# Attention of a two-layer kernel: an order written by hand gives way to a list scheduler, units of 512 queries and heads that share a bank

## The reference, cut to what matters

```python
q = _apply_rotary(q, cos, sin)
k = _apply_rotary(k, cos, sin)
attn = jnp.einsum('bhqd,bhkd->bhqk', q, k) * scale
allowed = (j <= i) & (i - j < WINDOW)
attn = jnp.where(allowed, attn, -jnp.inf)
attn = jax.nn.softmax(attn, axis=-1)
out = jnp.einsum('bhqk,bhkd->bhqd', attn, v)
```

## Time and profile before

| | |
|---|---|
| median of 3 runs | 2544.14 us (2537.84 to 2553.32) |
| the profiled execution | 2542.74 us, span 2541.0 us |
| TensorE busy | 1949.2 us, 77% of the span |
| VectorE, ScalarE, GpSimd busy | 1188.7, 837.3, 476.4 us |
| mean granted TensorE clock | 0.888 |
| the five attention stages | 1366.15 us, 54% of the span |

### The profile page before, as it was taken

The page is one execution under the profiler, slowest core; times in us unless marked ns, Lnnn a source line. Parts: engine busy times, 40 slices in busy tenths (PEclk is TensorE's granted clock), DMA queues, the critical chain, the costliest instruction groups (busy, mean ns, idle before and its releaser), DMA issues. The chain is left out here.

```text
span 2541.0 us, 32056 instructions
## 1 busy us (share of the span) xinstructions
PE 1949.2 (77%) x11444; PEld 1189.2 (47%) x11444; DVE 1188.7 (47%) x2913; ACT 837.3 (33%) x1671; POOL 476.4 (19%) x543
## 2 busy tenths in 40 slices
PE   5777688877667888767769797686797299999991
PEld 3455333345453333445433344564334266666660
DVE  4447666444656764436667543476774100000114
ACT  1332155533221645332126453221365122222212
POOL 4120211010202011103110110211100423333321
PEclk9889799988787999878889998797999599999995
DMA  6400330341003304410023123102210423333315
GB/s 162 52 2 1 66 43 10 51 51 34 2 2 65 51 1 52 51 35 1 26 41 51 25 34 46 34 0 46 30 27 1 145 63 70 70 69 67 69 19 145
DMA packets 91693, 115.01 MB, mean 45 GB/s; under 512 B 19616, under 2 KB 64864, under 8 KB 91376
## 3 DMA queue, kind: packets, MB, share of 16 engines
q1 hardware_dynamic: 76688, 96.07, 19.7%
q0 software_dynamic: 14848, 16.85, 4.0%
HBM read 40.72 MB, written 21.38 MB: 24 GB/s over the span
## 5 line engine op out<-in xcount | busy, mean ns | idle before, releaser
L419 ACT ACTIVATE b_probs<-b_psum 128x512 f32<-128x512 f32 (+3 forms) x768 | 348.7, 494 | 244.4 <-PE b_psum L363 237.9
L509 DVE TENSOR_REDUCE b_mneg<-b_psum 128x1 f32<-128x384 f32 (+3 forms) x512 | 240.7, 486 | 139.9 <-PE b_psum L341 135.4
L341 PE MATMUL b_psum<-b_qk 96*128 96x512 bf16 (+3 forms) x768 | 253.2, 350 | 40.1 <-DVE b_v L470 21.6
L538 POOL TENSOR_TENSOR b_rot<-b_product 128x128 f32<-128x128 f32 x256 | 111.3, 461 | 860.0 <-DVE b_product L464 860.0
L363 PE MATMUL b_psum<-b_qk 99*128 99x512 bf16 (+3 forms) x768 | 238.7, 332 | 10.4 <-DVE b_v L470 6.5
L504 DVE TENSOR_REDUCE b_mneg<-b_psum 128x2 f32<-128x384 f32 (+1 forms) x256 | 138.0, 541 | 228.6 <-PE b_psum L334 223.2
L391 PE MATMUL b_psum<-b_probs,b_v 128*32 128x192 f32 (+5 forms) x2688 | 235.5, 427 | 0.3
L1203 PE MATMUL b_psum<-b_w,b_hid 128*128 128x256 f32 x1024 | 222.4, 379 | 0.8 <-ACT b_hid L1227 0.8
L1248 DVE TENSOR_TENSOR b_ye<-b_psum,b_b2b 128x512 f32<-128x512 f32 x32 | 22.1, 692 | 428.9 <-PE b_psum L1203 390.5
L1194 PE MATMUL b_psum<-b_xgt,b_w 128*128 128x512 f32 x512 | 221.6, 593 | 0.0
L306 PE MATMUL b_psum<-b_wqkv,b_xt 128*128 128x384 f32 x512 | 204.9, 529 | 5.6 <-PEq L850 4.7
(11 more groups left out here) (201 smaller groups left out, 2939.8 us busy)
## 6 DMA issues: line engine op xcount, KB each, us to landing
b_qk<-b_split SPq DMA_DIRECT2D x324, 128.0 KB, 6.5
b_w<-in_W SPq DMA_DIRECT2D x16, 1024.0 KB, 7.0
b_qk<-b_split SPq DMA_DIRECT2D x120, 64.0 KB, 2.6
b_src<-in_x SPq DMA_DIRECT2D x4, 1024.0 KB, 5.5
normed<-b_probs SPq DMA_DIRECT2D x4, 1024.0 KB, 4.7
before_last_norm<-b_x SPq DMA_DIRECT2D x4, 1024.0 KB, 7.1
b_rows<-before_last_norm SPq DMA_DIRECT2D x8, 512.0 KB, 7.2
out<-b_rows SPq DMA_DIRECT2D x8, 512.0 KB, 3.0
```

The lines of the kernel that those rows point to most:

```text
L341: ins = pe.matmul(r[:, 0:e - a], q[0:KS, h, P * t:P * t + P], q[0:KS, HG + h, a:e], start=not last, stop=True, skip_group_check=True)
L419: act.activation(u.probs[t % 2][:, heads[0], a:e], u.psum[:, plan.bank[x], 0:e - a], ACT.Exp, scale=SCALE).then_inc(s.exp_done, 1)
L509: ins = dve.tensor_reduce(out, u.psum[:, plan.bank[x], 0:e - a], AX.X, ALU.max, negate=True)
L538: ins = pool.tensor_tensor(out[:, :, :, HALF * y:HALF * y + HALF], straight[:, :, :, HALF * y:HALF * y + HALF], crossed[:, :, :, HALF * (1 ...
```

## The change

A class `Plan` takes the place of `Script`. Its `describe` lists every step with its engine, a cost in us and the steps it waits for. `arrange` then plays these costs forward in time when the kernel is built: whenever an engine is free, it takes, among the kinds of step whose next one is ready, that with the longest chain of costs behind it. Each engine gets its own order (`plan.program`), and a step gets the bank that is free first, out of five (0, 1, 2, 3, 7). The costs are constants in the text, a DMA lands 3.0 us after its issue, and a wait across engines is 0.12 us.

Further: maxima, rows, exponentials, values and collect go by units of 512 queries (g, h) instead of a whole group; pieces of 128 columns hold four heads and pieces of 256 columns two, so that a causal group has 38 pieces for max and 38 for exp; a windowed group gets 9 cells and 18 pieces for exp instead of 8 and 16. The turned values share bank 6, two tiles at a time, where they had two banks and four tiles. The maxima of a unit go by one DMA from 12 rows. v has room for six groups, `mrow` and `mparts` are double; some small buffers of `route` now lie in `u.qk[1]`.

```diff
+    BANKS = (0, 1, 2, 3, 7)
+    TAKEN_BY = {"proj": "rotate", "fetch": "refill", "max": "reduce", "rows": "lines", "exp": "power", "out": "divide",
+              "back": "keep"}
+    LANDING = 3.0
...
+    def query_cells(self, g, h):
+
+        w = self.windowed[g]
+        return [(t, max(P * t, BANK * h), min(BANK * (h + 1), P * t + WQ if w else T))
+                for t in range(NT) if max(P * t, BANK * h) < min(BANK * (h + 1), P * t + WQ if w else T)]
+    def pieces(self, g, a, e):
+
+        n = 2 if self.windowed[g] else 4 if e - a <= P else 2 if e - a <= 2 * P else 1
+        return [(tuple(range(k, k + n)), a, e) for k in range(0, HG, n)]
...
+                add(("proj", j, t), "PE", 0.66, name("refill", 1, NC - 1) if j >= NG // 2 else None,
+                    name("load", 2 * j - 1, 1, 5, None) if t == 0 else None)
+                add(("rotate", j, t), "DVE", 0.98, ("proj", j, t), name("add", *divmod(n - 2, NT)) if n >= 2 else None,
+                    name("values", 2 * j - 5, 1, NT - 1) if j >= 3 else None)
+                add(("add", j, t), "POOL", 0.88, ("rotate", j, t), name("turn", *divmod(n - 2, NT)) if n >= 2 else None)
+                add(("turn", j, t), "PE", 0.25, ("add", j, t), name("rest", *divmod(n // 2 - 1, 4)) if t % 2 == 0 and n else None)
...
+        def load(g, y=None):
+            last = ("power",) + self.last_piece(g - 3, 1) if g >= 3 else None
+            q = 3 if y is None else 2 * y + 1
+            for part, kind in enumerate(("high", "mid", "low")):
+                for a in range(2):
+                    for slot in SLOTS_OF[a][part]:
+                        add(("load", g, a, slot, y), "SP", 0.46 if y is not None else 0.64, (kind, g // 2, q), last)
...
+                        add(("max", g, t, x), "PE", 0.03 + n * (w + (w if windowed[g] else P if mask else 0)) * 0.00042, y, z)
+                        add(("reduce", g, t, x), "DVE", 0.16 + n * w * 0.00103, ("max", g, t, x),
+                            name("parts", g - 1, h))
+            add(("parts", g, h), "DVE", 1.1, name("reduce", g, 4 * h + 3, self.pieces(g, *self.key_spans(g, 4 * h + 3)[-1])[-1]),
+                name("rows", *before(mine, 2)) if before(mine, 2) else None)
+            add(("rows", g, h), "PE", 0.25, ("parts", g, h))
+            add(("lines", g, h), "ACT", 0.6, ("rows", g, h), name("spread", *before(mine, 2)) if before(mine, 2) else None)
+            add(("spread", g, h), "SP", 0.5, ("lines", g, h))
...
+                    add(("exp", g, h, t, x), "PE", 0.03 + n * (w + (w if windowed[g] else P if mask else 0)) * 0.00042,
+                        ("spread", g, h))
+                    add(("power", g, h, t, x), "ACT", 0.18 + n * w * 0.00085, ("exp", g, h, t, x),
+                        name("values", *self.cells[i - 4]) if i >= 4 else None)
+                add(("values", g, h, t), "PE", 0.1 + (e - a) * 0.0017, ("power", g, h, t, x), name("collect", g - 1, h))
+            add(("collect", g, h), "ACT", 0.62, ("values", g, h, cells[-1][0]), name("out", g - 1, h))
+            add(("out", g, h), "PE", 0.45, ("collect", g, h))
+            add(("divide", g, h), "DVE", 0.75, ("out", g, h))
...
+            urgent[x] = st.cost + max([urgent[y] for y in followers[x]], default=0)
...
+        while left:
+            soonest, moved = None, False
+            for engine, lists in queues.items():
+                at = free_at.get(engine, 0.0)
+                best = None
+                for (q,) in lists:
+                    if not q:
+                        continue
+                    x = q[-1]
+                    if any(y not in done for y in steps[x].after):
+                        continue
+                    ready = max([done[y] + (0.0 if steps[y].engine == engine else self.LANDING if steps[y].engine == "SP"
+                                            else 0.12) for y in steps[x].after], default=0.0)
+                    if x[0] in self.TAKEN_BY:
+                        b = min(bank_free, key=lambda k: bank_free[k])
+                        ready = max(ready, bank_free[b])
+                    start = max(at, ready)
+                    if start > now:
+                        soonest = start if soonest is None else min(soonest, start)
+                    elif best is None or urgent[x] > urgent[best[0]]:
+                        best = (x, q)
+                if best is not None:
+                    x, q = best
+                    q.pop()
+                    left -= 1
+                    moved = True
+                    end = now + steps[x].cost
+                    free_at[engine] = done[x] = end
+                    self.program[engine].append(x)
+                    if x[0] in self.TAKEN_BY:
+                        b = min(bank_free, key=lambda k: bank_free[k])
+                        self.bank[x], self.after[x] = b, used.get(b)
+                        used[b] = x
+                        bank_free[b] = float("inf")
+                    if x in issue_of:
+                        bank_free[self.bank[issue_of[x]]] = end + 0.12
...
+    def in_bank(x, heads, w):
+
+        n = len(heads)
+        return u.psum[:, plan.bank[x], :].rearrange("p (h w) -> p h w", h=n)[:, :, 0:w]
...
-                    for j in range(3):
-                        sp.dma_start(u.qk[g % 3][KS + j:KS + j + 1, 0:HG, :].rearrange("o h (t q) -> o (h t) q", q=P),
-                                     u.mrow[32 * j:32 * j + 32, :]).then_inc(s.m_rows, 16)
+                    sp.dma_start(u.qk[g % 3][KS:KS + 3, 0:HG, BANK * h:BANK * h + BANK], u.mrow[n % 2][0:3 * HG, :]
+                                 ).then_inc(rows_sent[n % 2], 16)
...
+                    elif last:
+                        pe.matmul(out[:, :, P * t - a:P * t - a + P], u.id16[:, :],
+                                  u.causal_q[:, :].unsqueeze(1).broadcast_to([P, len(heads), P]), start=True, stop=True,
+                                  skip_group_check=True)
+                    for i, h in enumerate(heads):
+                        ins = pe.matmul(out[:, i, :], q[0:KS, h, P * t:P * t + P], q[0:KS, HG + h, a:e],
+                                        start=not last, stop=True, skip_group_check=True)
...
-    sbuf(nc, ctx, u, "v", [P, NG, NT, HG * (HD + 1) + 15])
+    sbuf(nc, ctx, u, "v", [P, 6, NT, HG * (HD + 1) + 15])
```

More of the change, by code:

```diff
@@ L232, in wait_bank @@
         y = self.after[x]
         if y is not None:
-            eng.wait_ge({"max": s.max_read, "exp": s.exp_done, "out": s.out_read, "proj": s.pj_read,
-                         "rows": s.rows_read, "fetch": s.fetched, "back": s.back_read}[y[0]], self.order[y] + 1)
+            pe.wait_ge({"proj": s.pj_read, "fetch": s.fetched, "max": s.max_read, "rows": s.rows_read, "exp": s.exp_done,
+                        "out": s.out_read, "back": s.back_read}[y[0]], self.order[y] + 1)
+SLOTS_OF = (((0, 1, 2), (3, 4), (5,)), ((0, 3, 5), (1, 4), (2,)))
@@ new lines, in rows_bank, with split_of, turned_bank, probs_of @@
+    def rows_bank(x):
+        return u.psum[:, plan.bank[x], :].bitcast(BF16)[0:3 * HG, 0:BANK]
+    def split_of(q, part):
+        return u.split[:, :, part, 2 * P * q:2 * P * q + 2 * P]
+    def turned_bank():
+        return u.psum[:, 6, :].rearrange("p (a x) -> p a x", a=2)
+    def probs_of(cell):
+        i = plan.cells.index(cell) % 4
+        return u.probs[i // 2][:, :, BANK * (i % 2):BANK * (i % 2) + BANK]
+    def unit_number(g, h):
+        return 2 * g + h
+    def load_done(eng, g, y=None):
+        if g:
+            eng.wait_ge(loaded[g], 16 * 2 * SLOTS)
+        else:
+            for n in range(2) if y is None else (y,):
+                eng.wait_ge(loaded[groups + n], 16 * 2 * SLOTS)
@@ L293, in _ @@
+            for n in range(2):
+                sp.wait_ge(rows_sent[n], 16 * groups)
             sp.wait_ge(later, 16 * len(LATER_WEIGHTS))
@@ L401, in _ @@
                     ins.then_inc(s.out_ready, 1)
+                elif kind == "back":
+                    y = x[2]
+                    pe.wait_ge(s.out_read, order[("divide", g + 1, y)] + 1)
+                    for t in range(4):
+                        ins = pe.transpose(u.psum[:, plan.bank[x], P * t:P * t + P], o_of(g)[:, 4 * y + t, 0:P], u.id32[:, :])
+                    ins.then_inc(s.back_ready, 1)
         @block.scalar
         def _(act):
-            for x in plan.steps:
+            for x in plan.program["ACT"]:
```

603 lines of the change are left out of this document (294 added, 309 removed).

## The result

The changed kernel takes **2340.8 us**, the median of 3 runs (2339.49 to 2347.63), where the kernel before took 2544.14. The ratio is 0.9205, with a 95% interval of 0.9152 to 0.9257: 203 us less, 8%. The profiled execution has a span of 2337.7 us (2541.0 before), a mean granted TensorE clock of 0.898 (0.888) and TensorE busy for 1912.0 us (1949.2).

What follows compares the result with a forecast made beforehand. Nothing was saturated: a joint stage needs about 224 us of TensorE and 117 are waiting. Savings of 134 us in three joint stages, 11 in the last and 19 in the first sum to 164, giving 2380, range 2265 to 2500.

Steps and rivals of the forecast that it cites:

- The head, 52: Start of a joint stage: first maxima at 22 us, first exponential at 52 us, 5 earlier than before.
- Group 0, to 99: First causal group of a joint stage: 37.7 us of work plus gaps of 0.25 a pair, 47 us.
- Group 1, 36 us, to 135: Second causal group of a joint stage: 29.2 us of work plus 38 gaps of 0.17 us, 36 us.
- Group 2, 53 us, to 188: Joint-stage group with fetch and pair 2: 43.1 plus 9.5 us, 53, where it was 65.4 with a stall of 8.33.
- The rest, 110: Joint stage after group 2: 130.9 us falls to 110, losing the 11.92 stall and about 9 through moved projections.
- Stages: Attention stage lengths: joint 298 us against 342.8 in the mean, last 193 (11 less), first 115 (19 less).
- causal groups over 45 us: Sign of being wrong: causal groups in the changed profile still taking over 45 us each.
- Outside the stages: Sign of being wrong: stages between the attention stages changing length at all.
- my lower rival, in which the gaps close further: Attention stages: five banks and planned order leave no gap, 2207 us, or about 2290 with half the gaps; chance 0.15.
- Pieces that share a bank: Causal groups: 38 pairs of max and exp pieces in place of 48, 1.7 us a group at 0.17 a pair.
- The rival of shrunken gain: Attention stages: wrong planner prices leave gaps and half the load stalls, 72 us gained, 2470 us; chance 0.17.
- The slower rival: Rows on SyncE stand behind late loads, 2656 us if all 22 are exposed, slower from 7.5 us a load; chance 0.11.

Runs made afterwards that it cites:

- e5: The changed kernel with four banks, one head a piece in causal groups and exponentials planned to wait for the whole group; 2431.8 us.
- e2: The changed kernel with pieces of causal groups back to one head each, 48 a group in place of 38; 2370.5 us.
- the combined kernel: Apparently the fastest run: the changed kernel with nearer prices, projections free to go ahead and rows first; 2262.7 us.
- e1: The changed kernel with four shared banks for the planner in place of five; 2429.1 us, 0.9527 of the kernel before.

## Why the prediction was right, and where its steps were not

The forecast was 2380 with a range of 2265 to 2500; it came out at 2341. The way and the range were right, and the gain was too small by a fifth: 164 us for 203. By its own steps, for the first joint stage:

- **The head, 52.** The first exponential came at 53.7, the first maxima at 21.9 (said: 22). The order held: 38 pieces and eleven more before the first exponential.
- **Group 0, to 99.** Its values end 101.4 us after the stage's start.
- **Group 1, 36 us, to 135.** They end at 135.0, 34 us for the group.
- **Group 2, 53 us, to 188.** They end at about 182, 47 us for the group. With 43.1 us of work the gaps are 4 and not 9.5: this term was mis-sized. The stalls of 8.33 and 11.92 before the maxima of windowed groups are gone from the joint stages. The 34.0 us at L449 are eight waits of 4 to 5 us before the first maxima of group 0 and of group 2 in the joint and last stages.
- **The rest, 110.** It took 104.5. TensorE is visibly idle there for only 2.7 us, and the clock is 1.00 where it was 0.89. The prediction read that the clock fell in the stall and gave it no term.
- **Stages.** Joint 286.5 for 298, last 192.4 for 193, first 118.7 for 115. The last stage is right by its parts as well: first exponential at 53.8, end of group 2 at 169.5 for 171. In the first I had the load of group 2 at 66 us; its maxima start at 72, after a wait of 4.80 for it.
- **VectorE** is busy for 184.5 us a joint stage (within 5 of 186). No wait in the attention stages that names a DMA is longer than 5.12 us. The sign that causal groups over 45 us would show me wrong was badly put, since my own sum has groups 0 and 2 above that.
- **Outside the stages** I had nothing, and named any change there as a sign of being wrong. It is 8 us, most of it after the last stage (593.7 to 589.3) and in the gap before it (147.1 to 143.4). What sets these I have not settled. Such stretches differ by as much within one execution (below), so the sign was too sharp.

The term that was mis-sized most is the gaps of group 2, with the rest of the stage behind it. I charged 0.17 to 0.32 us for each pair of a max and an exp piece and laid it all to two in-order engines that wait for each other. For group 1 this is not refuted: it took 33.7 us for the 29.2 that I counted as work, 0.12 a pair in place of 0.17. Only 0.6 of these 4.5 us are visible idle time (before, 2.3 of 8), since a wait that is shorter than the modelled tail of a matmul doesn't show. For the parts that hold projections the cause was in large part another. In group 2 of the kernel before 8.8 us were waits for the one bank in four that a projection held until VectorE had copied v, and in the head 5.5. Over the kernel these were 61.3 of 272.8 us of idle time, and 33.5 were the transposition of the maxima standing directly behind the last max piece in the list, once a group. Both went without the fifth bank (e5: 0.3 and 1.7 us). So my lower rival, in which the gaps close further, was right for group 2 and the rest, and my argument against it, which was made from group 1, did not speak for group 2. The view of waits by their releaser, read over the whole kernel, had both numbers before the change was made.

The second thing I left out was the price of being late by a little. "Pieces that share a bank" I valued at 1.7 us a causal group, 27 in all, and e2 says 30. But in e2 the lower clock can account for most of the growth, so the nearness of the two numbers may be luck. The half units, which I gave only the head, are worth 24; 21.7 us of waits for loads come back without them, by my reading because later exponentials release `u.qk` later.

The rival of shrunken gain had its premises right. Prices do matter: flat ones cost 81 us, nearer ones may gain 12, and with the projections let free 41. Its conclusion was wrong for the prices of this change. The slower rival had its mechanism right (waits for rows behind loads of up to 6.7 us with flat prices, and a 6.3 us landing with four banks). With the change's prices it stayed far from its turning point: other work stands between the issue of the rows and their use, 16 us of it at the place shown above, and over the whole kernel waits for rows are 4.0 us.

## What to carry to other kernels

Before charging a gap to the alternation of engines, sum TensorE's waits over the kernel by what ended them: a bank that waits for the second reader of another kind of step, or a small step that stands directly behind its producer in a shared list, shows there as many short waits. Then look part by part where these waits stand, and by the starts of the matmuls at what the view can't show. Measure the parts of a change together as well as apart: here a fifth bank was worth 36 or 88 us, and packing with half units 3 to 15 or 55, by whether the other was there. When a planner decides, take its prices from the trace first, the landing of small transfers behind large ones above all, and then look at what its dependencies forbid: one dependency and one rule of rank gave 66 us on top of the 12 for nearer prices, and the dependency alone, with the old prices, next to nothing.

## What was not expected of the hardware

The stretch between the first and the second joint stage has the same instructions in every kernel, yet it takes 146 to 155 us. Its windows in the changed kernel, with four banks and in the combined kernel:

```profile
538.92:689.18 150.26, 97.11 (x462) 79.18 (x461) 93.68 (x265) 31.66 (x59) 24.56 (x18) 0.80 0.05 15
```
```profile
563.20:718.50 155.30, 100.06 (x461) 81.27 (x460) 91.92 (x265) 31.55 (x59) 24.54 (x18) 0.77 0.05 15
```
```profile
515.40:661.40 146.00, 96.91 (x460) 78.34 (x460) 91.59 (x265) 31.66 (x59) 25.51 (x18) 0.81 0.05 16
```

The length goes with the granted clock. In the stretch of 15 us that starts 60 us after the attention stage's end the clock is 0.88 in the changed kernel and 0.63 with four banks, for nearly the same matmuls (43 and 39). The two passes of this stretch hold 11 of the 19 us by which these two profiled executions differ outside attention.

That the edit moved the clock there is not shown. The second pass of the same stretch is 150.2 us in the changed kernel and 156.3 with four banks, so each of these two executions repeats its length; but in the kernel before the two passes are 152.1 and 147.9, and e5, also with four banks, has 146.3 and 149.3. The execution of e1 that was profiled is also the longest of its four (2411 to 2433 us). So a single profile can hold 3% more or less in a stretch that no edit touched, and a difference of some 5 us there says nothing of the change. What makes the clock fall at one place and not at the other I could not tell from the records.
